# Eight matmuls into a free PSUM bank while the selection of experts is awaited

## Time and profile before

| what | us |
|---|---|
| median of 3 runs | 2759.8 |
| lowest and highest run | 2749.01, 2766.76 |
| profiled execution, its own time | 2745.8 |
| its span, first to last instruction | 2744.1 |
| PE busy in the span | 2365.1 (86%) |
| DVE busy, ACT busy | 1376.3, 1199.3 |
| mean granted clock of PE | 0.848 |

### The profile page before, as it was taken

The page is one execution under the profiler, slowest core; times in us unless marked ns, Lnnn a source line. Parts: engine busy times, 40 slices in busy tenths (PEclk is TensorE's granted clock), DMA queues, the critical chain, the costliest instruction groups (busy, mean ns, idle before and its releaser), DMA issues. The chain is left out here.

```text
span 2744.1 us, 55286 instructions
## 1 busy us (share of the span) xinstructions
PE 2365.1 (86%) x18441; PEld 1716.4 (63%) x18442; DVE 1376.3 (50%) x4993; ACT 1199.3 (44%) x2132; POOL 854.6 (31%) x883
## 2 busy tenths in 40 slices
PE   4999998888788987888788888988888918999997
PEld 2776666666566765666566666766666715666664
DVE  4465555555455544555556565655565333333332
ACT  3555444444344443454345454544444214444433
POOL 2213322223222222222222222222233133444443
PEclk7998878788788888898889898888898658999999
DMA  2010000000000000010001010000001204444444
GB/s 93 23 48 27 27 27 27 26 27 27 27 27 27 27 27 7 25 43 28 10 27 36 26 41 27 27 27 27 27 23 18 40 26 97 85 84 83 82 82 67
DMA packets 69872, 106.45 MB, mean 39 GB/s; under 512 B 25024, under 2 KB 29120, under 8 KB 69120
## 3 DMA queue, kind: packets, MB, share of 16 engines
q0 software_dynamic: 24096, 37.51, 7.9%
q1 hardware_dynamic: 45536, 65.69, 7.8%
HBM read 67.51 MB, written 35.65 MB: 38 GB/s over the span
## 5 line engine op out<-in xcount | busy, mean ns | idle before, releaser
L1089 PE MATMUL av<-vv,pr 128*128 128x17 f32 x4096 | 617.8, 287 | 6.0 <-issue 5.7
L1089 PEld LDWEIGHTS av<-vv,pr 128*128 128x128 f32 x4096 | 609.6, 227 | 19.9 <-issue 5.9
L519 ACT ACTIVATE pr<-st 128x512 f32<-128x512 f32 x512 | 305.0, 596 | 588.9 <-PE st L1075 444.7
L699 DVE TENSOR_REDUCE mx<-md 128x4 f32<-128x512 f32 x256 | 176.7, 690 | 343.8 <-remote 223.8
L1043 PE MATMUL md<-kk,qz 128*128 128x128 f16 x2048 | 212.4, 252 | 149.3 <-DVE mx L699 92.6
L1407 PE MATMUL y<-w1s,hgT 128*128 x1704 | 280.3, 315 | 4.7 <-ACT hgT L1321 4.7
L417 POOL DMA_INDIRECT lists<-row,posi x256 | 249.0, 973 | 86.2 <-issue 86.2
L1043 PEld LDWEIGHTS md<-kk,qz 128*128 128x128 f16 x2048 | 154.6, 114 | 182.0 <-issue 129.3
L702 DVE CUSTOM_DVE_ANT_0 md<-md,msk 128x128 f32<-128x128 f32 x1024 | 264.9, 321 | 0.0
L403 POOL TENSOR_TENSOR avs<-avs,rc 128x512 f32<-128x512 f32 x32 | 34.6, 1083 | 658.3 <-DVE rc L734 658.3
L1066 PE MATMUL st<-qz,kk 128*128 128x256 f16 x1024 | 211.9, 291 | 30.0 <-issue 22.4
(11 more groups left out here) (198 smaller groups left out, 3850.8 us busy)
## 6 DMA issues: line engine op xcount, KB each, us to landing
wst<-in_w SPq DMA_DIRECT2D x32, 352.0 KB, 3.6
cin<-in_ctx SPq DMA_DIRECT2D x32, 256.0 KB, 4.0
xin<-in_x SPq DMA_DIRECT2D x32, 256.0 KB, 3.8
xres<-in_x SPq DMA_DIRECT2D x32, 256.0 KB, 3.4
out<-x SPq DMA_DIRECT2D x32, 256.0 KB, 2.1
h_pairs<-ohs SPq DMA_DIRECT2D x32, 256.0 KB
lists<-row,posi POOLq DMA_INDIRECT x256
msk<-in_mask SPq DMA_DIRECT2D x32, 64.0 KB, 3.2
```

The lines of the kernel that those rows point to most:

```text
L519: act.activation(pr[:, path, :, :], st[path][:, :, :], ACT.Exp).then_inc(p_ex.sem, 1)
L699: dve.tensor_reduce(mx[:, 1, 4 * g:4 * g + 4], sm[1][:, :, :], AX.X, ALU.max).then_inc(s_ad.sem, 1)
L1089: i = pe.matmul(av[g // 2 % 2][:, h % 8, path, :], pr[:, path, j, :], vv[:, n.par, path, h, :], start=True, stop=True)
```

## The change

Before `places(c)` waits for `sel`, PE now issues eight matmuls: the 128x128 identity in float16 as the stationary operand and 512 columns of `wk` (the k projection's weights, which lie in SBUF for the whole attention part) as the moving one, each overwriting the whole bank `md[1]`. Nobody reads them. Two waits come ahead: that the logits of c were copied from the bank, and that all row maxima of b were taken. The calls in `last`, for the final two batches, keep the old form, so the eight are issued in 30 steps. Nothing changes on the other engines.

```diff
-        def places(n):
-
+        def places(n, running=None):
+
+            if running:
+                pe.wait_ge(r_lg.sem, r_lg.at(n))
+                pe.wait_ge(s_ad.sem, s_ad.at(running))
+                for c in range(2 * NC_):
+                    pe.matmul(md[1][:, :], ident16[:, :], wk[:, c % NC_, 0, :], start=True, stop=True)
             pe.wait_ge(r_sel.sem, r_sel.at(n))
             pe.matmul(md[1][:, 0:NE], tri[:, :], sel[:, :], start=True, stop=True)
             pe.matmul(md[1][:, NE:2 * NE], ones[:, :], sel[:, :], start=True, stop=True).then_inc(f_p.sem, 1)
@@
                 if u == 3 and c:
-                    places(c)
+                    places(c, b)
```

## The result

The changed kernel takes 2683.4 us (median of 4 runs, 2675.1 to 2693.8) where the kernel before takes 2760.1 (median of 4, 2749.0 to 2766.8): a ratio of 0.9728, 95% interval 0.9681 to 0.9775, 77 us less between the medians. A ratio compares executions within 1.5% of the fastest of their kernel and isn't the quotient of the medians beside it, which are of all executions; the profiles of **sixteen** and **both_four** are of executions beyond that bound. Profiled, the changed kernel has a span of 2679.4 us, 64.7 us under that of before, and a mean granted clock of 0.881 against 0.848.

What follows compares the result with a forecast made beforehand. PE's order of work bounds the kernel (busy 86%), slowed by clock falls behind the wait for `sel`. -62.7 + 5 + 1 + 3 = -54 us, from the median 2759.8 to 2706 us; 8-in-10 range 2684 to 2757.

Steps and rivals of the forecast that it cites:

- late part: From the router's projection to `w_v`: shorter steps shuffle where a second clock fall begins, -22 to +22 us, taken as 0.
- Falls gone: From the wait for `sel` to the router's projection: the clock stays full in 29 stretches, -62.7 us.
- Some falls remain: Nine steps with the 3.0 us wait: some may still fall, 0 to 14 us, a third taken, +5 us.
- The new wait: Before the router's projection: `router_weights` ends 0.7 us before DVE must copy values, so the whole gain arrives, 0 lost.
- Short waits: Three steps with waits of 1.0 to 1.5 us: the eight matmuls stick out by 0 to 0.6 us, about +1 us.
- The last step: The last step has no wait: the eight matmuls are wholly on the path, less what a sooner clock returns, +3 us.
- Not held: Behind the wait for `sel`: the eight matmuls don't hold the clock and all falls stay, 2764 us; chance 0.13.
- Late: At the wait for `sel`: the eight start at 1.2 GHz, outlast the wait, falls kept, 2793 us; chance 0.08.
- Given back later: Behind the router's projection: the gain is lost again in the paced part, 20 to 40 us, say 2740 us; chance 0.10.
- The Trainium skill's "<1%": Whole span: the skill's ramp penalty makes the falls worth under 27 us, result above 2732 us; the prediction followed the trace.

Runs made afterwards that it cites:

- sixteen: The changed kernel with sixteen of the matmuls in place of eight: 2490.5 us, ratio 0.9858 to the kernel before.
- both_four: The changed kernel with four matmuls, `places(c)` moved behind `values(b, 2)`, `h_turn` and `router` behind `values` in their u: 2501.8 us, ratio 0.9922.
- waits_only: The changed kernel with the two added waits kept and the eight matmuls left out: 2750.3 us, ratio 1.0046 to the kernel before.
- even_only: The changed kernel with the eight matmuls issued only where b is even: 2505.2 us, ratio 0.9958 to the kernel before.
- narrow: The changed kernel with 16 float32 matmuls of 17 columns in place of the eight: 2780.6 us, ratio 1.0174 to the kernel before.
- third group: The changed kernel unedited and three variants moving real work into the wait, on one quicker chip; unedited 2484.1 us against 2519.1, ratio 0.9914.
- four: The changed kernel with four of the matmuls in place of eight: 2451.1 us, ratio 0.9695 to the kernel before.
- after_again: The changed kernel unedited, run and profiled again: 2671.1 us against 2735.4 for the kernel before, ratio 0.9738.
- turned: The changed kernel with 32 float16 transposes of 128x128 on PE in place of the eight matmuls: 2674.4 us, ratio 0.9787.

## Why the prediction came out as it did

The mechanism was right: a wait of 2.2 or 3.0 us is followed by a fall of the clock, work behind it at half rate costs 1.6 to 3.1 us a step, and eight unread matmuls in the wait prevent it, in all 29 steps of the first profile and in 24 of 29 in each of the next two. **waits_only** and **even_only** show that the matmuls do it and that they do it in their own step, **narrow** that filling the time isn't enough. The size was off: 54 us forecast, 65 between the profiled executions, 77 between the medians, and the measured 2683.4 lies 0.6 us under the lower end of the range, 2684. That end was drawn too tight: the forecast's own range of 2686 to 2728 used some 15 us for the late part where the text bounds it by 22, and with 22 it would have gone from 2679 to 2737. Of the 77 us, 12 are the choice of executions: the one profiled before was 14 us under its median, the one after 2 us. For the other 65, term by term:

- *Falls gone, -62.7.* The full-clock stretch was put at 13.65 us; it is 13.58. The fall itself was worth 458.63 - 29 x 13.58 = 64.8 us.
- *Some falls remain, +5.* None in the first profile, five (6 us) in the second and again in the third. A fair size, but not of a kind that could be told ahead: in all three profiles the same 1.3 us stay idle in the longer waits, and the clock falls behind some of them and not behind others.
- *The new wait, 0.* This step failed, though the sum hides it. I had written that DVE ends `router_weights` with 0.7 us of room before it is asked for the values, and that the whole gain reaches the router's projection. 26 of 29 stretches are 0.47 us longer than 13.58: 12.2 us lost. The two timelines of DVE and of POOL show it, the kernel before first:

```profile
1970.17 0.17 DVE L841 CAST posi<-pos 128x8 int32<-128x8 f32 x1
```

```profile
1970.24 2.13 POOL L377 TENSOR_TENSOR ks<-t,ks 128x1024 f16<-128x1024 f32 x1 [1.26 <-ACT ks L497]
```

and the changed kernel:

```profile
1913.12 2.15 DVE L841 CAST posi<-pos 128x8 int32<-128x8 f32 x1
...
1915.58 0.44 DVE L729 COPY avs<-av 128x272 f32<-128x272 f32 x1 [0.20 <-DVE tok L844]
```

```profile
1913.10 2.14 POOL L377 TENSOR_TENSOR ks<-t,ks 128x1024 f16<-128x1024 f32 x1 [1.17 <-ACT ks L497]
```

  Line 841 works on 128x8 values. Before, it started 0.07 us ahead of POOL's long subtraction and took 0.17 us. In the changed kernel POOL starts 0.02 us ahead of it, since ACT hands over `ks` some 0.08 us sooner after line 1121, and line 841 takes 2.15 us, until POOL is done. DVE is through with `router_weights` 6.8 us behind line 1121 and no longer 4.8, while the values are there after 5.5: the 0.7 us of room became 1.3 us of lateness, and `ohs` is late for PE. The steps bear it out one by one: line 841 takes 0.17 us in the three steps whose stretch is 13.58 us, and 2.08 to 2.15 us in the 26 others. Over all steps the instruction's shortest, median and longest duration in ns are, before and after:

```profile
L841 DVE CAST posi<-pos x32: 171/172/2142, 186.4 to 2233.4; 128x8 int32<-128x8 f32 x32
```

```profile
L841 DVE CAST posi<-pos x32: 172/2094/2148, 192.7 to 2171.3; 128x8 int32<-128x8 f32 x32
```

- *Short waits, +1.* Nothing sticks out in this profile: some idle time is left ahead of line 1121 in all 29 steps, 0.06 us at the least and 0.3 or more in all but two.
- *The last step, +3.* The sign was wrong. From `max_turn` to line 1121 it takes 2.0 us more, as reckoned, but the stretch behind takes 12.62 us where it took 17.85 at a low clock: 3.3 us less in all. What a held clock gives back there was put far too small.
- *The late part, 0, bounds -22 to +22.* It gave 4.6 us in the first pair of profiles, and two profiles of the changed kernel on slower chips differ by 22 us in it. There the bounds held. On the quicker chips they were too narrow: a step there takes 20.4 or 26.2 us by whether the late fall comes, up to 6 us x 29.
- *The measured sum.* -64.8 (falls) + 12.2 (the new wait) - 3.3 (last step) - 4.6 (late part) leaves 4.2 us less elsewhere, for 64.7 in all. That the total came within 11 us of the forecast is in part luck: a wait that was missing from it, 12.2 us, is offset by terms that turned out better.
- *The rivals.* "Not held" is out (clock 1.00 in all 29 stretches). "Late" is out for eight matmuls, and real for sixteen and for **narrow**. "Given back later" isn't seen on the slower chips; on the third group's chip the gain is 22 us by the ratio and 35 between the medians, not 77, while the stretches behind line 1121 are as short as on the others. There is no profile of the kernel before on a quicker chip, so that the rest went to more late falls is argued and not shown.
- *The Trainium skill's "<1%"* ("TensorE: Matmul & The Clock Gate", Part 1). The sentence stands in the page's account of the warm-up at a kernel's start, and the prediction held it against falls that come back in every step. Those behind this one wait were worth 2.4% of the span, so it isn't to be used for them.

Open stay: why **four** did better than eight by ratio (it had fewer long steps late, on another of the quicker chips), why the filler gains 2.7% on the slower chips and about 1% on the third group's, and what makes the late fall come or not.

## What to carry to other kernels

Read a wait of PE together with the granted clock behind it: a wait that is bound by another engine can cost more in the work that follows than in itself, and then filling it with wide matmuls can pay though it shortens nothing. Here it paid 2.7% on the slower chips and about 1% on the quicker one where it was run. A busy PE isn't the test of a filler, the granted clock behind it is: eight float16 matmuls of 512 columns held it here and sixteen float32 ones of 17 columns, longer in time, didn't. And it has to be shorter than the wait: sixteen matmuls in place of four outlasted it and took 39 us more. On the one chip where both were run, real work moved into the wait did as well as eight matmuls, and both tricks together did worse than either. Where a step has a second fall of its own, moving PE earlier deals it anew, and a gain of 2 to 3% from the first can shrink or vanish there; measure on more than one chip.

## What was not expected of the hardware

- Some of DVE's small instructions take until a long one of POOL ends, if that started before them. Line 841 takes 0.17 us alone and 2.15 beside POOL's 128x1024 subtraction (2.13 us). Lines 843 and 844 don't: they took 0.15 and 0.14 us within that subtraction in the kernel before. Which start comes first decides, by a few hundredths of a microsecond. In the profiles of the kernel before, of the result, **after_again**, **turned** and **four**, each of the 98 executions of line 841 that began 0.01 to 0.07 us behind the subtraction took over 2 us and ended 0.02 to 0.03 us behind it; each of the 62 others took 0.17. In the selection chain that the filler covers, line 800 takes 2.0 us in most steps and ends with POOL's other subtraction (median 2.08, shortest 0.17). So some two of the 2.2 or 3.0 us of waiting look like POOL's doing; no run moved POOL's work to test it.
- Transposes hold PE's clock as matmuls do: 4096 columns of either give stretches of 412 and 411 us and ratios of 0.974 and 0.979.
- The same program takes 2735 to 2760 us on some chips and 2516 to 2519 on others. The profiles differ in stand-stills of DVE labelled "remote" (223.8 us against 8.2). The one of the earlier trace rows lies within POOL's indirect DMAs, but one of 10.70 us ends at 1059.60 us, and the last of these that POOL issued in that step had ended at 1044.70. So what they are stays open.
